# Cross attention and a LoRA mixture in fp32: two TensorE transposes per tile replaced by VectorE block transposes with SBUF-to-SBUF transfers, pair scores one step sooner, softmax ahead of the router

## The reference, cut to what matters

```python
# x (8, 1024, 1024), ctx (8, 64, 1024), mask (8, 64), all fp32
def xattn(h, mem, mask):                       # h is the layernorm of x
    scores = einsum('bsd,bmd->bsm', h, mem) / sqrt(1024)
    scores = where(mask[:, None, :], scores, -1e30)
    attn = softmax(scores, axis=-1)
    return where(any(mask), einsum('bsm,bmd->bsd', attn, mem), 0)

def ffn(x, weight, lora_A, lora_B, router_w):  # 8 experts of rank 16, top 2
    base = einsum('btd,od->bto', x, weight)
    probs = softmax(einsum('btd,ed->bte', x, router_w))
    vals, idx = top_k(probs, 2); vals = vals / vals.sum(-1, keepdims=True)
    w = dense(vals, idx)                       # (tokens, 8), two non-zeros each
    Ax = einsum('nd,erd->ner', x, lora_A)
    return base + einsum('ner,ne,eor->no', Ax, w, lora_B) * 2

x = x + xattn(layernorm(x), ctx, mask)
x = x + ffn(layernorm(x), weight, lora_A, lora_B, router_w)
```

## Time and profile before

| | |
|---|---|
| median of 3 runs | 1066.97 us (1066.63 to 1070.31) |
| the profiled execution | 1066.78 us, span of its instructions 1065.0 us |
| PE busy | 1057.3 us (99%) |
| PEld busy | 1039.6 us (98%) |
| DVE busy | 796.1 us (75%) |
| ACT busy | 492.0 us (46%) |
| POOL busy | 104.5 us (10%) |
| granted TensorE clock | 1.000 |
| packets and bytes of DMA | 105407 packets, 148.93 MB |

### The profile page before, as it was taken

The page is one execution under the profiler, slowest core; times in us unless marked ns, Lnnn a source line. Parts: engine busy times, 40 slices in busy tenths (PEclk is TensorE's granted clock), DMA queues, the critical chain, the costliest instruction groups (busy, mean ns, idle before and its releaser), DMA issues.

```text
span 1065.0 us, 18645 instructions
## 1 busy us (share of the span) xinstructions
PE 1057.3 (99%) x6198; PEld 1039.6 (98%) x6198; DVE 796.1 (75%) x2113; ACT 492.0 (46%) x959; POOL 104.5 (10%) x278
## 2 busy tenths in 40 slices
PE   8999999999999999999999999999999999999998
PEld 7999999999999999999999999999999999999998
DVE  6967787777777777777777778767777778777673
ACT  7744544444444544444544445444454444454330
POOL 3210110101101101101011011011010010110100
PEclk9999999999999999999999999999999999999999
DMA  8435444555455454544455444554445644345322
GB/s 312 166 120 163 124 142 109 165 146 144 131 137 139 132 163 122 169 111 133 145 143 165 134 102 137 163 155 138 107 130 150 174 136 130 99 142 163 85 88 79
DMA packets 105407, 148.93 MB, mean 140 GB/s; under 512 B 43280, under 2 KB 78224, under 8 KB 105360
## 3 DMA queue, kind: packets, MB, share of 16 engines
q1 hardware_dynamic: 104496, 146.94, 47.8%
q10 hardware_dynamic: 864, 1.45, 0.4%
HBM read 78.74 MB, written 33.55 MB: 105 GB/s over the span
## 4 chain that ended last, share of the span: by engine, by line
PE 96%; DVE 2%; DMA 1%; POOL 0%; issue 0%; ACT 0%; ACTq 0%; DVEq 0%; POOLq 0%
PE base_ps L963 28%; PE base_ps L965 28%; PE base_ps L964 28%; PE s_ps L990 3%; PE ro_ps L1027 3%; PE s_ps L991 3%; PE ro_ps L1028 3%; DMA xT_raw<-in_xT 1%; PE ro_ps L1016 1%; PE ro_ps L1012 1%; DVE w_lo L302 0%; DVE x L772 0%; DVE stats L778 0%; DVE xT_lo L729 0%; POOL w_lo L302 0%
## 5 line engine op out<-in xcount | busy, mean ns | idle before, releaser
L963 PE MATMUL base_ps<-w_hi,xT_hi 128*128 128x388 f32 x1512 | 523.9, 347 | 0.0
L965 PE MATMUL base_ps<-w_hi,xT_lo 128*128 128x388 f32 x1512 | 512.4, 339 | 0.0
L964 PE MATMUL base_ps<-w_lo,xT_hi 128*128 128x388 f32 x1512 | 512.0, 339 | 0.0
L963 PEld LDWEIGHTS base_ps<-w_hi,xT_hi 128*128 128x128 f32 x1512 | 284.3, 188 | 6.6
L964 PEld LDWEIGHTS base_ps<-w_lo,xT_hi 128*128 128x128 f32 x1512 | 285.3, 189 | 2.5
L965 PEld LDWEIGHTS base_ps<-w_hi,xT_lo 128*128 128x128 f32 x1512 | 284.4, 188 | 0.0
L790 DVE STREAM_TRANSPOSE x2T<-xq 128x512 f32<-128x512 f32 x122 | 123.2, 1087 | 7.2 <-DMA xq<-xn 7.1
L431 POOL TENSOR_TENSOR rstd<-var_eps,neg_half 128x1 f32<-128x1 f32 x64 | 35.1, 548 | 884.3 <-DVE var_eps L783 884.3
L489 ACT ACTIVATE x2T<-x 128x1024 f32<-128x1024 f32 x63 | 66.9, 1062 | 115.4 <-DMA x<-in_x 96.0
L535 ACT CAST xT_hi<-x2T 128x512 fp32r<-128x512 f32 x122 | 69.7, 619 | 66.2 <-DVE x2T L790 66.2
L529 ACT ACTIVATE xn<-x,shift,rstd 128x1024 f32<-128x1024 f32 x61 | 75.7, 1241 | 51.1 <-POOL shift L434 50.4
(11 more groups left out here) (110 smaller groups left out, 1189.7 us busy)
## 6 DMA issues: line engine op xcount, KB each, us to landing
out<-x SPq DMA_DIRECT2D x63, 512.0 KB, 2.7
xT_raw<-in_xT SPq DMA_DIRECT2D x62, 512.0 KB, 5.4
x<-in_x SPq DMA_DIRECT2D x62, 512.0 KB, 3.3
xq<-xn SPq DMA_DIRECT2D x244, 128.0 KB, 3.6
h<-w_raw SPq DMA_DIRECT2D x248, 16.0 KB, 2.4
ctx_raw<-in_ctx SPq DMA_DIRECT2D x7, 520.0 KB, 6.4
w_raw<-in_wT SPq DMA_DIRECT2D x8, 386.0 KB, 8.7
ctxT_raw<-in_ctxT SPq DMA_DIRECT2D x7, 256.0 KB, 7.0
```

What stands on the lines that cost most here:

```text
L963: pe.matmul(out_, a_hi, w_h, start=start, stop=False, skip_group_check=again)
L964: pe.matmul(out_, a_hi, w_l, start=False, stop=False, skip_group_check=again)
L965: return pe.matmul(out_, a_lo, w_h, start=False, stop=stop, skip_group_check=again)
```

## The change

For the tiles from the fifth on, both transposes through the array go. In place of `scores`, DVE transposes the pair's scores in 32x32 blocks from `s_ps` into SBUF (`s_transposes`, `sq`), and four DMAs on SP's queue (`s_exchange`) put the blocks where they belong (`s_raw`); `softmax_scores` reads `s_raw`. `pair_scores` is made one step sooner (for t+3 and t+4 in odd steps, before for t+2 and t+3 in even ones), inside group 2 of the base product. In place of `e_transpose`, DVE transposes `e_split` in blocks (`e_transposes`, `eq`), and four DMAs (`e_exchange`), two on ACT's queue and two on SP's, build `e_raw`, from which ACT makes `eT`. On DVE `softmax_scores` of t+2 stands at the head of the step, before `router_top`, and `softmax_split` with `e_transposes` before `router_gate`. On SP the store of x comes first in a step. The host lays out xT and ctx so that rows fall in the order that the block transposes leave. `xT_high` and the ctx preparation move by a step with the pair scores. The buffers are parts of `w_raw[0]`, which is free after the opening.

```diff
         hq = w_raw[0][:, C - 1, 0:P]
+        eq = w_raw[0][:, C - 1, P:2 * P]
+        e_raw = w_raw[0][:, C - 1, 2 * P:3 * P]
+        sq = w_raw[0][:, C - 2, 0:T2]
+        s_raw = w_raw[0][:, C - 3, 0:T2].rearrange("p (i k c) -> p i k c", i=Q, k=2)
...
+        def e_exchange(engine, tile, i0):
+            engine.wait_ge(eq_done, count(tile, 1, 1 - 4))
+            for i in range(i0, i0 + 2):
+                engine.dma_start(e_raw[:, i * QP:(i + 1) * QP], eq[i * QP:(i + 1) * QP, :]).then_inc(e_loaded, 16)
...
+            def s_exchange(tile):
+                sp.wait_ge(sq_done, pairs(tile, 1, 1 - 2))
+                for i in range(Q):
+                    sp.dma_start(s_raw[:, i].rearrange("p k c -> p (k c)"),
+                                 sq[i * QP:(i + 1) * QP, :]).then_inc(s_loaded, 16)
             def step(tile, first=False):
                 b, j = tile
+                store(tile)
                 if exists(after(tile, 2)) and not first:
                     exchange(after(tile, 2))
+                if exists(after(tile, 3)) and not first:
+                    e_exchange(sp, after(tile, 3), 2)
                 if exists(after(tile, 1)) and not first:
                     h_exchange(after(tile, 1))
-                store(tile)
...
-                if j % 2 == 0 and exists(after(tile, 6)):
-                    sp.wait_ge(xT_split, pairs(after(tile, 2), 2, 2))
-                    load_xT(after(tile, 6))
+                if j % 2 == 1 and exists(after(tile, 7)):
+                    sp.wait_ge(xT_split, pairs(after(tile, 3), 2, 2))
+                    load_xT(after(tile, 7))
+                if j % 2 == 0 and exists(after(tile, 4)):
+                    s_exchange(after(tile, 4))
...
             def eT_copy(tile):
+                act.wait_ge(e_loaded, count(tile, 16 * Q, 16 * Q * (1 - 4)))
+                act.wait_ge(readout_done, count(tile, 2))
+                act.copy(eT[:, :], e_raw).then_inc(eT_copied, 1)
...
# step(tile) of ACT
                     norm2(nxt)
+                if exists(nxt2):
+                    softmax_exp(nxt2)
                 gate_exp(tile)
-                if j % 2 == 0 and exists(nxt2):
-                    sT_copy(nxt2)
+                if exists(nxt2):
+                    e_exchange(act, nxt2, 0)
...
-                if j % 2 == 0 and exists(after(tile, 4)):
-                    for i in range(2):
-                        xT_high(after(tile, 4), i)
-                if exists(nxt2):
-                    softmax_exp(nxt2)
...
                     x2T_high(nxt)
+                if j % 2 == 1 and exists(after(tile, 5)):
+                    for i in range(2):
+                        xT_high(after(tile, 5), i)
...
+            def e_transposes(tile):
+                dve.wait_ge(e_split_done, count(tile, 1, 1))
+                dve.transpose(eq, e_split[:, :].bitcast(f32)).then_inc(eq_done, 1)
+            def s_transposes(tile):
+                dve.wait_ge(sT_done, pairs(tile, 1, 1))
+                dve.transpose(sq.rearrange("p (j k c) -> p k j c", k=2, c=QP),
+                              s_ps[:, 0:T2].rearrange("p (k j c) -> p k j c", k=2, c=QP)).then_inc(sq_done, 1)
...
# step(tile) of DVE
+                if exists(nxt2):
+                    softmax_scores(nxt2)
                 router_top(tile)
+                if exists(nxt2):
+                    softmax_split(nxt2)
+                    e_transposes(nxt2)
                 router_gate(tile)
                 h_transposes(tile)
-                if exists(nxt2):
-                    softmax_scores(nxt2)
-                    softmax_split(nxt2)
...
                     for i in range(TS):
                         x2_transposes(nxt, i)
+                if j % 2 == 1 and exists(after(tile, 3)):
+                    s_transposes(after(tile, 3))
                 hT_low(tile)
...
# step(tile) of PE
                 base(tile, 0, range(C))
...
-                if j % 2 == 0 and exists(nxt2):
-                    pair_scores(nxt2)
-                base(tile, 1, range(4))
-                if exists(nxt2):
-                    scores(nxt2)
-                base(tile, 1, range(4, C))
-                base(tile, 2, range(3))
-                if exists(nxt2):
-                    e_transpose(nxt2)
-                base(tile, 2, range(3, 5))
+                base(tile, 1, range(C))
+                base(tile, 2, range(2))
+                if j % 2 == 1 and exists(after(tile, 3)):
+                    pe.wait_ge(sq_done, pairs(after(tile, 3), 1, -2))
+                    pair_scores(after(tile, 3))
+                base(tile, 2, range(2, 5))
                 if exists(nxt2):
                     readout(nxt2)
                 base(tile, 2, range(5, C))
```

More of the change, by code:

```diff
@@ L513, in softmax_exp, with eT_copy, first_softmax_exp @@
                 act.wait_ge(softmax_step, count(tile, 5, 3))
+                act.wait_ge(eq_done, count(tile, 1, -4))
+                act.activation(e_all[:, :], s_all[:, :], ACT.Exp, bias=neg_max[:, :],
+                               accum_out=e_sum[:, :]).then_inc(exp_done, 1)
+                act.activation(e_split[:, 0:M], s_all[:, :], ACT.Exp, bias=neg_max[:, :]).then_inc(exp_done, 1)
+            def eT_copy(tile):
+                act.wait_ge(e_loaded, count(tile, 16 * Q, 16 * Q * (1 - 4)))
+                act.wait_ge(readout_done, count(tile, 2))
+                act.copy(eT[:, :], e_raw).then_inc(eT_copied, 1)
+            def first_softmax_exp(tile):
+                act.wait_ge(softmax_step, count(tile, 5, 3))
                 act.wait_ge(e_split_done, count(tile, 1))
@@ L518, in softmax_exp, with first_eT_copy @@
                                accum_out=e_sum[:, :]).then_inc(exp_done, 1)
-                act.activation(e_split[:, 0:M], s_all[:, :], ACT.Exp, bias=neg_max[:, :]).then_inc(exp_done, 1)
-            def eT_copy(tile):
+                act.activation(first_e(0), by_blocks(s_all[:, :]), ACT.Exp, bias=neg_max[:, :]).then_inc(exp_done, 1)
+            def first_eT_copy(tile):
                 act.wait_ge(eT_done, count(tile, 1, 1))
@@ L623, in _ @@
             xT_high((0, 0), 1)
-            softmax_exp((0, 0))
+            first_softmax_exp((0, 0))
             w_high(0, 0)
-            eT_copy((0, 0))
+            first_eT_copy((0, 0))
             for r in range(1, WPARTS):
@@ L634, in _ @@
             w_high(1, 2)
-            softmax_exp((0, 1))
+            first_softmax_exp((0, 1))
             w_high(1, 3)
-            eT_copy((0, 1))
+            first_eT_copy((0, 1))
             w_high(2, 0)
@@ L650, in _ @@
             b_high()
-            softmax_exp((0, 2))
+            first_softmax_exp((0, 2))
             first_hT_high((0, 0))
-            eT_copy((0, 2))
+            first_eT_copy((0, 2))
             norm1_mean((0, 3))
@@ L659, in _ @@
             first_norm2((0, 2))
-            softmax_exp((0, 3))
+            first_softmax_exp((0, 3))
             first_x2T_high((0, 2))
             first_hT_high((0, 1))
-            eT_copy((0, 3))
+            first_eT_copy((0, 3))
+            for i in range(2):
+                xT_high((0, 6), i)
             for j in range(2, TPB):
@@ L743, in softmax_scores, with first_softmax_scores @@
                 b, j = tile
+                k = j % 2
                 if j % TPB == 0:
                     dve.wait_ge(mask_step, b * 3 + (j // TPB * 3 + 3))
+                dve.wait_ge(rstd1_done, count(tile, 1, 1))
+                dve.wait_ge(s_loaded, pairs(tile, 16 * Q, 16 * Q * (1 - 2)))
+                dve.scalar_tensor_tensor(out=by_blocks(s_part[:, :]), in0=s_raw[:, 2:4, k, :], scalar=rstd1[:, :],
+                                         in1=by_blocks(mask_bias[:, :]), op0=ALU.mult, op1=ALU.add)\
+                   .then_inc(softmax_step, 1)
+                dve.wait_ge(softmax_step, count(tile, 5, 1))
+                dve.scalar_tensor_tensor(out=by_blocks(s_all[:, :]), in0=s_raw[:, 0:2, k, :], scalar=rstd1[:, :],
+                                         in1=by_blocks(s_part[:, :]), op0=ALU.mult, op1=ALU.add)\
+                   .then_inc(softmax_step, 1)
+                dve.wait_ge(softmax_step, count(tile, 5, 2))
+                dve.tensor_reduce(out=neg_max[:, :], in_=s_all[:, :], axis=AX.X, op=ALU.max,
+                                  negate=True).then_inc(softmax_step, 1)
+            def first_softmax_scores(tile):
+                if tile == (0, 0):
+                    dve.wait_ge(mask_step, 3)
                 dve.wait_ge(rstd1_done, count(tile, 1, 1))
@@ L893, in step @@
                     norm2_stats(nxt2)
+                if j == TPB - 3 and exists((b, TPB)):
+                    mask(b + 1)
             def add_bases(tile):
@@ L1184, in by_contraction, with by_blocks, by_fourths @@
         return np.ascontiguousarray(a.T.reshape(d // P, P, n).transpose(1, 0, 2))
+    def by_blocks(a):
+        n, d = a.shape
+        return np.ascontiguousarray(a.reshape(4, n // 4, d).transpose(1, 0, 2).reshape(n, d))
```

(7 more changed lines are left out.)

54 lines of the change are left out of this document (34 added, 20 removed).

## The result

The changed kernel takes **1057.29 us** (median, 1056.82 to 1057.63), the kernel before 1066.87 on the same chip (1066.63 to 1070.31): ratio 0.9902, 95% interval 0.9882 to 0.9923. That is 9.6 us faster; 12.1 were forecast. The profiled execution took 1056.82.

The account below looks back on a forecast made before the run. The prediction took PE's instruction stream as the bound. Removing both transposes from 60 tiles, 60 x (0.103 + 0.100) = 12.2 us, took the profiled 1066.78 to 1054.6, or 1054.8 as a median; range 1053 to 1067.

Parts of the forecast that it names:

- PE's stream is the bound, and a removed slot is given back: PE's instruction stream sets the time; a removed instruction gives back its share of the distance of starts while others' slack holds.
- 0.103 + 0.100 us for the transposes: On PE, the two transposes' cost per tile, read from distances of matmul starts; over 60 tiles 12.2 us.
- Rival 4: On PE, the transposes cost their duration of about 275 ns, making the time 1034; chance 0.03.
- The pair's move at zero: On PE, moving the 16 pair matmuls into group 2 of odd steps costs nothing; upper bound 6 us.
- The loop at 15.5, under the step's 16.04: The chain from one add_bases start on DVE to the next takes 15.5 us, under the mean step of 16.04.
- A from 0.4 to 0.8, up to 1.5: Time of add_bases' start on DVE in a step: 0.4 to 0.8 us, up to 1.5 with a batch's context work.
- eT at A + 8.2: eT is ready 8.2 us after add_bases' start, at most 9.7 us into a step, against readout at 11.15 in even steps.
- xT_low to the pair as the tightest slack: On DVE, xT_low ends at 8.7 us of a step; PE's pair matmuls need it at 9.55: 0.85 us of slack.
- All deadlines hold, so no term but the 12.2 remains: Every input reaches PE in time, so new waits add nothing to the 12.2 us gain.
- Rival 2: New PE waits, from late xT_low, eat a part: 6 us (1061), or 1067 with the group's split; chance 0.22.
- the full gain: The whole 12.2 us comes off PE, giving 1053.5 to 1058 us; chance 0.62.
- Rival 3: Small packets delay h's landing, the add_bases loop exceeds 16.04 and PE waits every step: 1071 to 1090; chance 0.13.

Follow-up runs that it names:

- Experiment 1: The changed kernel with two transposes of a constant, read by nobody, put back on PE at the old places in each of 60 steps: 1070.31 us, ratio 1.0035.
- experiment 2: The changed kernel with the pair's matmuls one chunk (0.53 us) later in group 2 of odd steps: 1056.17 us, ratio 0.9901.
- 10: The changed kernel with ctx_high ahead of e_exchange on ACT's queue in the seventh step of each batch: 1054.78 us, ratio 0.9892.
- 7: The changed kernel with four more 16 KB DMAs of a constant per step, issued by ACT right behind its two of e: 1090.02 us, ratio 1.021.
- Experiment 6: The changed kernel with softmax behind the router again on DVE, and likewise on ACT and SP: 1129.88 us, ratio 1.0587.
- 8: The changed kernel with four more 16 KB DMAs per step, issued by ACT behind ctx_high and ctxT_high, just ahead of eT_copy: 1071.17 us, ratio 1.0034.

## Why the prediction was right, and where it was not

- **PE's stream is the bound, and a removed slot is given back:** right. Experiment 1 shows it from the other side: the slots back, the time back.
- **0.103 + 0.100 us for the transposes:** mis-sized. Measured 0.245 a tile, 14.7 us for 12.2. In undisturbed steps (from 530.25 before, from 415.58 after) the offset between the two kernels is 0.10 right behind the first transpose, 0.13 some 15 matmuls later, and 0.24 behind the second, where it stays. The readings at the spot missed what the first transpose does to the matmuls after it; why these drift is open. The step distance holds it all.
- **Rival 4, the duration as price (1034):** excluded; 120 transposes added 13 us, not 33. The measurement decides against reading the 275 ns of the Trainium skill (TensorE: Matmul & The Clock Gate, Part 4: PE-mode transpose) as a price in a full stream; as a duration it agrees with the 0.27, though it stands on the page beside a figure for bf16 and the transposes here are fp32.
- **The pair's move at zero:** right. Steps of 15.04 and 16.95, and 16.96 in the last steps of experiment 2, leave nothing for a split of the group; their upper bound of 6 us is out.
- **The loop at 15.5, under the step's 16.04:** right, 15.4.
- **A from 0.4 to 0.8, up to 1.5:** wrong. Single even steps reach 0.44, but odd ones are at 1.7 to 2.1 once the kernel has settled, last steps of batches at 2.85, and the early tiles 3 to 17 go up to 2.8 as well. Two things were missed. The e issues can't begin at A + 4.85 when A is low, for e's block transpose stands behind MAX, and MAX behind PE at 4.56; the prediction had e's transpose at about 6.0 for ACT's issues, but did not carry it into the loop. They begin at 5.97, h's at 7.51 (tile 34, whose A is 0.55), and by the loop's own terms (3.95 + 0.3 + 0.65 + 1.21 + 3.24) the next A is 16.86 - 15.04 = 1.8; it was 1.73. And in the seventh step ctx_high stands behind ACT's issues, which were only checked for eT, hT_high and x2T_high (experiments 10 and 7).
- **eT at A + 8.2:** the step that failed most. Its landing was taken from h, 2.4 us; e landed in 3.3 to 3.6. h, too, was issued straight behind xq before the change, but the 2.4 is the median over its four pieces, and the spread was in the trace. One line's view of h's issues before gives least, median and most:

```profile
DMA to landing us min/median/max: 1.8/2.4/3.5
```

Taken by their place in the group, the four pieces landed in 3.2, 2.7, 2.3 and 1.9 us (medians of 62 groups): however soon a piece was issued, it landed only behind xq. SP's two pieces of e, which now have the first two places, took 3.6 and 3.1. eT was ready at A + 9.2, which at A above 1.9 is past an even readout at 11.11. Experiment 6 shows the cause, since there e landed in 1.9.
- **xT_low to the pair as the tightest slack:** right, and it was used up, 0.12 us in each last step of a batch (experiment 2). "All deadlines hold, so no term but the 12.2 remains" was the sentence that failed: 4.7 us of waits remain.
- **Rival 2 (new waits eat a part)** named the right mechanism, but eT's share was the larger and the whole was under its price of 6. That the time lies in the range of the full gain is in part luck: of two errors, 2.5 us more gain and 4.7 us of waits, one covers half of the other.
- **Rival 3 (the loop becomes the bound through small packets)** did not occur: h landed faster than before, 1.9 against 2.4; it is issued 1.35 us behind the end of xq's issues now (423.11 and 421.76), where it stood straight behind them. Experiments 7 and 8 show the way there. The Trainium skill's rule on transfers under 512 bytes (DMA: Bandwidth & Descriptors, opening table) stood in the prediction for this rival. The same page of the Trainium skill (DMA: Bandwidth & Descriptors, Why small descriptors are slow) says that transfers from SBUF to SBUF don't suffer the penalty of small descriptors, so for these pieces the rule was a weak support; that 34560 more of them slow h is what experiments 7 and 8 show. Whatever such a transfer costs by itself is inside the 1.9 us, and no run here separates it.
- **DVE at 79% and not binding:** right, 78%; the pair's block transpose took 0.42, not 0.57.

## What to carry to other kernels

Price an instruction in a full stream by the distance of whole steps, or put dummies back and time them; neither its duration nor the gap beside it is the price. When a path goes over DMA, take the landing time from a transfer of the same place in its group, with the same transfers still under way on any queue, and not from a median over the group. And when a wait or an issue is put on an engine, list everything behind it in every kind of step, the rare ones too: three small moves of lines were worth 3.9 us here, more than a third of the change itself.

## What the runs showed of the hardware

- Equal pieces of 16 KB in rows of 128 bytes landed in 1.9 us when xq's 512 KB had landed, and in 3.3 to 3.6 with them under way, on ACT's queue (3.6) no less than on SP's behind xq (3.3). With 34560 more small packets h went from 1.9 to 2.7.
- SP's two issues of e took 1.25 to 1.5 us as a rule, but 1.86 in tile 16 and 2.56 in tile 15. ACT issued its two within 0.5 us of them there, but so it did in the step shown above, where they took 1.26: the cause is open.
- A 128x128 fp32 transpose of 0.27 us duration cost 0.12 us of a full PE stream; of the first one in a step, 0.03 did not show at its place.
